# Splitting the mask pass of a top-p attention kernel between VectorE and GpSimd on Trainium2

## The chip, the cores and the metric

The kernel runs on one core of a Trainium2 chip. The metric is the device time of one execution in microseconds (us). Three runs of the kernel before took 1435.52, 1439.35 and 1441.99 us, so the median is 1439.35 us. Engines carry the names that the profile gives them: PE (TensorE), PEld (its weight loads), DVE (VectorE), ACT (ScalarE), POOL (GpSimd), SP (the queue of the loads).

## The reference, cut to what matters

```python
def top_p_attention(X, W1, W2, W3):          # X: 3327 x 128
    logits = (X @ W1.T @ W2.T) @ (X @ W3.T).T
    probs = softmax(logits)                  # 3327 x 3327
    # keep the largest probabilities of a row until their sum reaches 0.9
    keep_sorted = cs - sp < 0.9              # sp sorted, cs its running sum
    A = probs * mask
    return A / max(A.sum(-1), 1e-12)

R = row-normalised (adj + identity)
for n in range(2):                           # steps one and two
    A  = top_p_attention(Xa, W1, W2, W3)
    Xf = R @ Xf ;  Xa = A @ Xa
    Z += Xf @ U1[n].T + Xa @ U2[n].T
h = X + Z ; layer norm with gain and bias ; x + that ; layer norm
```

## The kernel before, in words

The 3327 rows are padded to 3328 and cut into 26 tiles of 128 rows; two tiles make a pair, so there are 13 pairs in each of the two steps (in the code `s` is 0 or 1, `p` the pair, `t` the tile, `x` or `xx` the tile within the pair). A tile of attention holds 128 x 3328 numbers in fp32. Two buffers `E01` and, in step one, a third hold pairs of such tiles.

**The life of a pair.** PE computes the logits in 7 chunks of up to 512 columns (line 550) and ACT stores them in `E` (line 667). DVE takes the 8 largest of each run of columns (line 833), gets the row's maximum and posts it (line 858). ACT then replaces candidates and rows by exponentials (lines 686 and 691) and posts `e_ready`. On this DVE's `search` (lines 913 to 1018) looks for the threshold `TSTAR` of each row among the candidates; while it waits for its own results it already takes the maxima of the next pair. It needs some 30 us to `TSTAR` (line 987). Where rows of a pair could not be settled (a flag tells), `level` (line 1036) reads the tiles again; that is the case for pairs 0, 5, 6, 8, 9 and 10 of step two. Before the masks, DVE finishes the next pair's maxima, so that ACT can start on the next pair's exponentials.

**The masks.** `settle` (line 1218) does this for both tiles of a pair: in step two four `match_replace` of 832 columns each (line 1232) put zeros in place of surplus ties, then one `scalar_tensor_tensor` over all 3328 columns (line 1234) multiplies the numbers by "at or above `TSTAR`", adds up what it keeps into `SUM`, and posts `a_ready`. After both tiles line 1283 takes the inverse of `SUM`.

**Units of PE's work.** PE's work is a list of units, each of 7 chunks: an A unit multiplies one masked attention tile by the features, an R unit one tile of the adjacency matrix. For each chunk PE turns up to four 128 x 128 blocks (line 595), ACT copies them out of PSUM (line 716, a ring of 3 buffers in this stage), and PE multiplies two chunks later (line 616). In step two a pair's body is A, A and then four or three R units (`STEP_R`, line 64; four for even pairs, three for odd ones, none for pair 12). The logits of pair p + 2 are made in the body of pair p, and its exponentials come at the end of that body (from step 36 on, line 166), when ACT is through with the copies before. All of this is one fixed order for each engine: an ACT instruction that waits holds everything that ACT does after it.

**Work that is spread out.** When the last unit of a pair of output tiles is done, the layer norms of these two tiles start: 6 rounds, one for each following unit (`norm_rounds`, lines 181 to 193). ACT does its half of a round at chunk 2 of the unit (lines 794 to 796), POOL its half in `norm_round` (line 485) after `add_part` of the unit before. ACT's round 0 waits for `h_taken`, that is for POOL's `add_part` (line 479) of the unit that ended the pair (line 757); a later round waits for POOL's half of the round before (line 759).

The units around the pairs that matter here, as the planner numbers them: pair 6 has its A units at 69 and 70. Before them stand the R units 66, 67 and 68. At chunk 2 of unit 68 ACT has round 4 of output pair 0 and round 0 of output pair 1; unit 67 is the one that ended output pair 1. Pair 10 has its A units at 91 and 92, with the R units 88, 89 and 90 before them; at chunk 2 of unit 90 ACT has round 4 of output pair 7 and round 0 of output pair 8, which unit 89 ended. For the even pair 8 (units 80 and 81) unit 79 has no round 0. For the odd pairs 7 and 11 a round 0 stands in the unit before the A units as well (units 74 and 96, after units 73 and 95). At chunk 0 of unit 102, the first A unit of pair 12, ACT has round 2 of output pair 11, which waits for POOL's round 1 (seven instructions, lines 493 to 499).

POOL's own program follows the units in their order (lines 510 to 520): the identity is added to the next R tile (`add_diagonal`, line 441), then the unit's result is saved (step one) or added (`add_part`), then its rounds come.

Of the kernel before, what the change touches and what calls it, by code (L numbers as in the profile page):

```python
# [6 lines left out]
def gnn_top_p_kernel(nc, x, adj, W1, W2, W3, U1, U2, ln_g, ln_b, out):  # L7
# [6 lines left out]
    P = 128  # L14
# [32 lines left out]
    MATCH = 4  # L47
    MW = NP // MATCH
    SLOTS = PARTS * 8
    SUB = 16  # L50
# [6 lines left out]
    QW = NP // QUARTERS  # L57
    HALF = [NP // 2, N - NP // 2]


# [119 lines left out]

    ROUNDS = 6
    LATE_EVERY = 3
    norm_rounds = {}
# [6 lines left out]
    for k in sorted(norm_rounds):  # L190
        norm_rounds[k].sort(key=lambda job: (job[1] if k > last_part.k else 0))
        for job in norm_rounds[k]:
            norm_at[job] = len(norm_at)
    a_unit = {(u.s, u.t): u for u in units if u.kind == "A"}

# [12 lines left out]
    with ctx:  # L208
# [6 lines left out]
        def sem(name):  # L215
            return ctx.enter_context(nc.semaphore(name))
# [62 lines left out]
        part = sb("part", [P, 2, SUB])  # L279
        st = sb("st", [P, 64])  # L280
        mv = sb("mv", [P, NT])
        sd = sb("sd", [P, NT])
# [42 lines left out]
        e_ready = sem("e_ready")  # L325
        a_ready = sem("a_ready")
        diag_ready = sem("diag_ready")
        blk_ready = sem("blk_ready")
# [87 lines left out]
        def _(pool):  # L416
# [68 lines left out]
            def norm_round(p, r):  # L485
# [14 lines left out]
                elif r == 2:  # L500
# [4 lines left out]
                    pool.tensor_tensor(h, h, X0[:, t, 0:D], ALU.add).then_inc(pool_round, 1)  # L505

            add_diagonal(r_units[0])
            add_diagonal(r_units[1])
            pool.wait_ge(h_loaded, 48)
            for u in units:  # L510
                if u.kind == "R" and 1 < u.n + 1 < 2 * NT and u.n + 1 != START_R:
                    add_diagonal(r_units[u.n + 1])
                if u.kind == "A" and u.s == 0 and u.t == NT - 1:
                    add_diagonal(r_units[START_R])
                if u.turned:
                    save(u)
                elif u.k <= last_part.k:
                    add_part(u)
                    for job in norm_rounds.get(u.k + 1, ()):
                        norm_round(*job)  # L520

        @block.tensor
        def _(pe):
# [286 lines left out]
        def _(dve):  # L810
# [49 lines left out]
            class Chain:  # L860
# [15 lines left out]

            (Z, DROPZ, THR, LOW, PICK, BUDGET, LOWW, ROOM, TSTAR, GAP, SLOW, S2, FLOOR, FLOOR2, TIE, TOTAL, TIES, CUT,
             LO, HI, WIDTH, L2, TN, GN, COUNT, LEAST, STEP, SUM, COARSE_LO, NEXT) = range(30)

            def two(n):  # L880
# [31 lines left out]

            def search(link, s, par):
                n = NC[s]
# [272 lines left out]
            for s in range(STEPS):  # L1187
                runs.finish()
                for p in range(NPAIR):
# [9 lines left out]
                    link = Chain(s_search, runs, fill, 8 if s else 0)  # L1199
                    search(link, s, par)  # L1200

# [15 lines left out]

                    def settle():

                        link = Chain(s_tie)  # L1220
                        if s:
                            link(v.tensor_tensor(gone[:, :, :, :], rank[:, :, :, :],
                                                 excess[:, :, :].rearrange("p x (n a) -> p x n a", a=1).to_broadcast([P, 2, MATCH, 8]),
                                                 ALU.is_le))
                            flat = "p x n k -> p x (n k)"
                            link(v.tensor_tensor(gone[:, :, :, :].rearrange(flat), gone[:, :, :, :].rearrange(flat),
                                                 wide(two(TSTAR), 8 * MATCH), ALU.mult))
                        for xx in range(2):
                            if s:
                                for k in range(MATCH):  # L1230
                                    back = e[:, xx, k * MW:(k + 1) * MW][:, ::-1]
                                    link.post(v.match_replace(back, gone[:, xx, k, :], back, 0.0))  # L1232
                                dve.wait_ge(s_tie, link.n)
                            v.scalar_tensor_tensor(out=e[:, xx, :], in0=e[:, xx, :], scalar=one(TSTAR, xx), in1=e[:, xx, :],  # L1234
                                                   op0=ALU.is_ge, op1=ALU.mult, accum_out=one(SUM, xx)).then_inc(a_ready, 1)

# [5 lines left out]
                    with dve.If(code > 0):  # L1242
                        if s:
# [27 lines left out]
                            with dve.If(left > 0):  # L1271
                                by_tile()
                                settle()
                        else:
# [70 lines left out]
```

## Time and profile before

| what | value |
|---|---|
| median of three runs | 1439.35 us |
| the profiled execution's own time | 1437.9 us |
| its span in the trace | 1436.1 us |
| PE busy | 1229.3 us (86%) |
| DVE busy | 1288.7 us (90%) |
| ACT busy | 921.2 us (64%) |
| POOL busy | 354.1 us (25%) |
| chain that ended last, by engine | PE 44%, DVE 37%, ACT 11%, issue 5%, POOL 1% |

Times in the trace are in us from the start of the span. "Idle before" is an engine's idle time ahead of an instruction, and the name behind the arrow is what ended it. The chain that ended last is followed back from the last instruction.

### The profile page before, as it was taken

To read this page: it belongs to the slowest core of one execution; us is meant where nothing else is said; L and a number is where in the kernel's file an instruction comes from. 1 tells how busy PE (TensorE), PEld (TensorE's weight loads), DVE (VectorE), ACT (ScalarE), POOL (GpSimd) and SP (SyncE) were. 2 spreads that over 40 slices of the span, in tenths; PEclk is the share of its full clock that TensorE was granted. 3 is DMA by queue.
4 is the path that set the end of the run, shared out by engine and by line. 5 is a ranking of instruction groups with operands and counts; after the bars stand their busy time and mean duration, and the time that the engine had idled before them with its cause. 6 is when DMAs were issued, how large, how long until landed. Compare 5 with 4: busy or idle time off the path is not lost.

```text
span 1436.1 us, 29717 instructions
## 1 busy us (share of the span) xinstructions
PE 1229.3 (86%) x9162; PEld 1037.9 (72%) x9162; DVE 1288.7 (90%) x7002; ACT 921.2 (64%) x1974; POOL 354.1 (25%) x584
## 2 busy tenths in 40 slices
PE   7899999999997989997999796919894965929896
PEld 3677777777785977887888786818784765828796
DVE  5799889988984898999989999899999998999995
ACT  4887888788757555755575655636664635636764
POOL 0221232123200341313141220202332312312242
PEclk9999999999998999998999898959997997969998
DMA  5000000000021440412132131211412031211311
GB/s 204 1 2 2 2 2 2 2 2 2 2 97 48 151 184 11 182 49 96 54 139 96 48 134 60 97 48 49 144 49 96 16 129 49 86 59 50 144 49 48
DMA packets 16599, 96.49 MB, mean 67 GB/s; under 512 B 1251, under 2 KB 8930, under 8 KB 9730
## 3 DMA queue, kind: packets, MB, share of 16 engines
q1 hardware_dynamic: 16384, 94.14, 18.6%
q8 instruction: 72, 1.18, 0.3%
q14 instruction: 143, 1.17, 0.3%
HBM read 92.43 MB, written 1.70 MB: 66 GB/s over the span
## 4 chain that ended last, share of the span: by engine, by line
PE 44%; DVE 37%; ACT 11%; issue 5%; POOL 1%; DVEq 1%; DMA 0%; SPq 0%; ACTq 0%; POOLq 0%
PE bank L616 25%; DVE cand L833 13%; PE bank L595 11%; DVE junkC L890 8%; PE bank L550 5%; ACT E L691 4%; DVE E L1232 2%; ACT blkT L716 2%; ACT cand L686 2%; DVE sub L1054 2%; DVE E L1234 1%; PE bank L631 1%; DVE junkS L890 1%; DVE slots L953 1%; ACT S L691 1%
## 5 line engine op out<-in xcount | busy, mean ns | idle before, releaser
L716 ACT ACTIVATE blkT<-bank 128x512 f32<-128x512 f32 (+1 forms) x728 | 406.7, 565 | 283.0 <-PE bank L595 279.0
L833 DVE MAX8 cand<-E 128x8 f32<-128x32 f32 (+1 forms) x2992 | 404.4, 192 | 37.2 <-ACT E L667 22.7
L616 PEld LDWEIGHTS bank<-X,blkT 128*128 128x128 f32 x2704 | 330.3, 192 | 107.8 <-ACT blkT L716 76.3
L616 PE MATMUL bank<-X,blkT 128*128 128x129 f32 (+1 forms) x2704 | 377.5, 282 | 13.9 <-ACT blkT L716 12.7
L595 PE MATMUL bank<-ident,S 128*128 128x128 f32 x1560 | 243.3, 276 | 16.0 <-POOL S L447 14.2
L595 PE MATMUL bank<-ident,E 128*128 128x128 f32 x1144 | 182.1, 284 | 81.9 <-DVE E L1234 81.9
L890 DVE SCALAR_TENSOR_TENSOR junkC<-cand,st 128x128 f32<-128x128 f32 (+2 forms) x390 | 241.1, 626 | 2.4
L616 PE MATMUL bank<-YF,blkT 128*128 128x128 f32 x1352 | 193.0, 287 | 43.1 <-ACT blkT L716 43.1
L616 PEld LDWEIGHTS bank<-YF,blkT 128*128 128x128 f32 x1352 | 172.5, 199 | 74.7 <-ACT blkT L716 63.6
L550 PE MATMUL bank<-kT,Q 64*128 64x512 f32 (+1 forms) x728 | 197.2, 614 | 7.9 <-ACT E L667 7.6
L595 PEld LDWEIGHTS bank<-ident,E 128*128 128x128 f32 x1144 | 142.8, 148 | 84.0 <-DVE E L1234 82.8
L595 PEld LDWEIGHTS bank<-ident,S 128*128 128x128 f32 x1560 | 187.2, 143 | 21.1 <-POOL S L447 16.3
L667 ACT ACTIVATE E<-bank 128x512 f32<-128x512 f32 (+1 forms) x308 | 158.0, 567 | 57.0 <-PE bank L550 56.7
L616 PE MATMUL bank<-YA,blkT 128*128 128x128 f32 x1352 | 185.5, 280 | 0.5 <-ACT blkT L716 0.5
L616 PEld LDWEIGHTS bank<-YA,blkT 128*128 128x128 f32 x1352 | 170.5, 197 | 1.0 <-ACT part_h L737 0.7
L1234 DVE SCALAR_TENSOR_TENSOR E<-E,st 128x3328 f32<-128x3328 f32 x44 | 163.0, 3721 | 8.8 <-DVE flag_i L1031 6.8
L691 ACT ACTIVATE E<-E,negm 128x1664 f32<-128x1664 f32 x88 | 147.4, 1675 | 0.0
L476 POOL TENSOR_TENSOR H<-hy,H 128x128 f32<-128x128 f32 x26 | 37.9, 1456 | 283.7 <-ACT hy L752 283.7
L1232 DVE MATCH_REPLACE8 E<-gone,E 128x832 f32<-128x832 f32 x104 | 103.8, 1009 | 0.0
L686 ACT ACTIVATE cand<-cand,negm 128x520 f32<-128x520 f32 (+1 forms) x78 | 44.9, 591 | 90.7 <-DVE negm L858 90.7
L550 PEld LDWEIGHTS bank<-kT,Q 64*128 64x128 f32 x728 | 56.8, 186 | 42.9 <-issue 27.4
L483 POOL TENSOR_TENSOR H<-part_h,H 128x128 f32<-128x128 f32 x50 | 33.2, 664 | 190.1 <-ACT part_h L737 190.0
(222 smaller groups left out, 1336.2 us busy)
## 6 DMA issues: line engine op xcount, KB each, us to landing
S<-in_adj_dram SPq DMA_DIRECT2D x50, 1663.5 KB, 7.0
S<-in_adj_dram SPq DMA_DIRECT2D x2, 1455.6 KB, 8.1
X<-in_x_dram SPq DMA_DIRECT2D x6, 256.0 KB, 4.1
out_dram<-H SPq DMA_DIRECT2D x1, 1408.0 KB
S<-in_adj_dram SPq DMA_DIRECT2D x2, 194.9 KB, 9.9
u_in<-in_L_gnn_U_dram SPq DMA_DIRECT2D x4, 64.0 KB, 9.5
out_dram<-H SPq DMA_DIRECT2D x1, 128.0 KB
w_in<-in_L_gnn_W_dram SPq DMA_DIRECT2D x2, 32.0 KB, 2.0
```

What stands on the lines that cost most here:

```text
L476: pool.tensor_tensor(H[:, u.t, :], hy[:, z, 0:D], H[:, u.t, :], ALU.add)
L550: pe.matmul(lg_banks(q)[xx][:, 0:LW[c]], Q[h0:h1, p, :], kT[h0:h1, s, c * BANK:c * BANK + LW[c]], start=True, stop=True).then_inc(logits_r ...
L595: m = pe.transpose(BLK[early][slot][:, b * P:(b + 1) * P], src[:, j * P:(j + 1) * P], ident[:, :])
L616: m = pe.matmul(bank[int(u.acc)][:, 0:width], blkT[:, slot, b * P:(b + 1) * P], rhs[:, j, 0:width], start=(j == 0), stop=(j == NT - 1))
L667: act.activation(E[where_e[s, p]][:, xx, c * BANK:c * BANK + LW[c]], lg_banks(q)[xx][:, 0:LW[c]], ACT.Copy).then_inc(logits_done, 1)
L686: act.activation(c, c, ACT.Exp, bias=negm[:, par, xx:xx + 1], scale=1.0, accum_out=total[:, par, xx:xx + 1])
L691: return act.activation(e[:, xx, lo:hi], e[:, xx, lo:hi], ACT.Exp, bias=negm[:, par, xx:xx + 1], scale=1.0, accum_out=Zh[:, par, xx, half: ...
L716: act.activation(blkT[:, slot, 0:w], BLK[early][slot][:, 0:w], ACT.Copy).then_inc(blk_done, 1)
L833: v.max(cand[:, par, xx, 8 * r:8 * r + 8], E[where_e[self.s, self.p]][:, xx, r * w:min((r + 1) * w, N)]).then_inc(s_max, 1)
L890: return v.scalar_tensor_tensor(out=out, in0=a, scalar=limit, in1=a, op0=ALU.is_lt, op1=ALU.mult, accum_out=total)
L1232: link.post(v.match_replace(back, gone[:, xx, k, :], back, 0.0))
L1234: v.scalar_tensor_tensor(out=e[:, xx, :], in0=e[:, xx, :], scalar=one(TSTAR, xx), in1=e[:, xx, :], op0=ALU.is_ge, op1=ALU.mult, accum_out= ...
```

## The change

In step two, POOL masks the last 320 columns (`EW`) of each tile, with two instructions and a buffer `over`; DVE masks the first 3008. DVE does the `match_replace` of the last quarter first and posts `end_cleaned` with it. PE waits for `end_masked` at chunk 5 of an A unit, the first that touches these columns. DVE waits for the masks of the pair before ahead of writing `TSTAR` again. In POOL's program `mask_ends(p)` stands two units ahead of the pair's first A unit, between that unit's `add_diagonal` and its save or `add_part`. The kept sum is no longer added up by the mask pass: it is the row's mass minus the allowed drop, minus the gap, minus the ties taken out. A fallback for rows that `level` leaves open keeps adding up (`settle(False)`). Step one stays as it was.

```diff
+    EW = 5 * P // 2
...
+    MASKS_AHEAD = 2
...
+    masks_before = {a.k - MASKS_AHEAD: a.pair for a in units if a.kind == "A" and a.s and a.x == 0}
...
+            def mask_ends(p):
+                for t in (2 * p, 2 * p + 1):
+                    pool.wait_ge(end_cleaned, t + 1)
+                    last = E[where_e[1, p]][:, t % 2, NP - EW:]
+                    limit = st[:, 2 * TSTAR + t % 2:2 * TSTAR + t % 2 + 1]
+                    if t:
+                        pool.wait_ge(end_masked, t)
+                    then(pool.tensor_scalar(over[:, :], last, limit, None, ALU.is_ge))
+                    pool.tensor_tensor(last, last, over[:, :], ALU.mult).then_inc(end_masked, 1)
...
             for u in units:
                 if u.kind == "R" and 1 < u.n + 1 < 2 * NT and u.n + 1 != START_R:
                     add_diagonal(r_units[u.n + 1])
+                if u.k in masks_before:
+                    mask_ends(masks_before[u.k])
...
+                if u.s and u.kind == "A" and c == (NP - EW) // BANK:
+                    pe.wait_ge(end_masked, u.t + 1)
...
+                if s and p:
+                    dve.wait_ge(end_masked, 2 * p)
                 link(v.tensor_reduce(two(TSTAR), d, AX.X, ALU.min))
...
+                        link.post(v.tensor_tensor(two(SUM), two(Z), two(DROPZ), ALU.subtract))
...
+                            for k in (MATCH - 1, *range(MATCH - 1)):
                                 back = e[:, xx, k * MW:(k + 1) * MW][:, ::-1]
+                                ins = v.match_replace(back, gone[:, xx, k, :], back, 0.0)
+                                if k < MATCH - 1 or not counted:
+                                    link.post(ins)
+                                else:
+                                    ins.then_inc(end_cleaned, 1)
+                                if xx == 0 and counted:
+                                    if k == 0:
+                                        link.post(v.tensor_tensor(two(SUM), two(SUM), two(GAP), ALU.subtract))
+                                        link.post(v.tensor_reduce(two(S2), gone[:, :, :, :].rearrange(flat), AX.X, ALU.add))
+                                        total_at = link.n
+                                    elif k == 1:
+                                        dve.wait_ge(s_tie, total_at)
+                                        link.post(v.tensor_tensor(two(SUM), two(SUM), two(S2), ALU.subtract))
+                            dve.wait_ge(s_tie, link.n)
...
+                            ins = v.scalar_tensor_tensor(out=e[:, xx, 0:end], in0=e[:, xx, 0:end], scalar=one(TSTAR, xx),
+                                                         in1=e[:, xx, 0:end], op0=ALU.is_ge, op1=ALU.mult,
+                                                         accum_out=None if counted else one(SUM, xx))
+                            ins.then_inc(a_ready, 1)
```

## Rows read from the trace of the kernel before

**Rows 1.** Window, length; busy us (count) of PE, PEld, DVE, ACT, POOL; clock; DMA.

```profile
805.00:1290.00 485.00, 358.65 (x2743) 317.47 (x2743) 456.85 (x2627) 269.60 (x611) 113.77 (x222) 0.87 0.21 75
```

**Rows 2.** Waits, same stretch: waiter, awaited, us in total, times, longest.

```profile
ACT cand L686 <- DVE negm L858: 82.3, 5, 22.9
...
PE bank L595 <- DVE E L1234: 77.0, 3, 31.2
```

**Rows 3.** Timeline of DVE, pair 6: start, us, engine, line, operation, operands.

```profile
966.23 1.01 DVE L1232 MATCH_REPLACE8 E<-gone,E 128x832 f32<-128x832 f32 x1
...
970.25 3.69 DVE L1234 SCALAR_TENSOR_TENSOR E<-E,st 128x3328 f32<-128x3328 f32 x1
...
974.66 0.17 DVE L931 TENSOR_SCALAR st<-st 128x2 f32<-128x2 f32 x1
974.73 0.16 DVE L932 TENSOR_SCALAR st<-st 128x2 f32<-128x2 f32 x1
```

**Rows 4.** Timeline of PE at the start of unit 69.

```profile
966.29 2.82 PE L595 MATMUL bank<-ident,E 128*128 128x128 f32 x12 [31.18 <-DVE E L1234]
```

**Rows 5.** Timeline of ACT at the end of pair 6's body.

```profile
1040.38 0.19 ACT L691 ACTIVATION_READ_ACCUMULATOR E<-E,negm 128x1 f32 x1
```

**Rows 6.** Timeline of DVE at the start of the search for pair 8.

```profile
1040.71 0.16 DVE L929 TENSOR_TENSOR st<-Zh 128x2 f32<-128x2 f32 x1
```

**Rows 7.** Groups of DVE by shape: line, names, shapes, count, busy us, mean ns.

```profile
L890 DVE SCALAR_TENSOR_TENSOR junkC<-cand,st 128x832 f32<-128x832 f32 x104 | 113.0, 1096 | 1.3
```

**Rows 8.** Timeline of POOL: 128 columns, the first beside a mask pass of DVE.

```profile
603.22 3.30 POOL L471 TENSOR_SCALAR scaled<-hy,row_inv 128x128 f32<-128x128 f32 x1 [3.64 <-ACT hy L752]
...
658.88 0.46 POOL L472 TENSOR_TENSOR H<-scaled,H 128x128 f32<-128x128 f32 x1
659.32 0.60 POOL L473 TENSOR_SCALAR YF<-hy,row_inv 128x128 f32<-128x128 f32 x1
```

**Rows 9.** Timeline of POOL: a two-input instruction of 256 columns.

```profile
984.22 0.73 POOL L504 TENSOR_TENSOR H<-H,gb 128x256 f32<-128x256 f32 x1
```

**Rows 10.** Timeline of DVE at 602 us.

```profile
602.35 3.69 DVE L1234 SCALAR_TENSOR_TENSOR E<-E,st 128x3328 f32<-128x3328 f32 x1
```

**Rows 11.** Timeline of ACT: unit 68, chunk 2, then pair 7's exponentials.

```profile
931.93 0.31 ACT L764 ACTIVATE u_in<-H 128x128 f32<-128x128 f32 x1
...
932.53 0.85 ACT L716 ACTIVATE blkT<-bank 128x512 f32<-128x512 f32 x2
...
957.30 0.84 ACT L686 ACTIVATE cand<-cand,negm 128x520 f32<-128x520 f32 x1 [21.72 <-DVE negm L858]
```

**Rows 12.** Timeline of POOL: add_part of unit 67.

```profile
927.88 0.46 POOL L483 TENSOR_TENSOR H<-part_h,H 128x128 f32<-128x128 f32 x1 [4.15 <-ACT part_h L737]
```

**Rows 13.** Timeline of PE at the lower clock.

```profile
1023.55 1.92 PE L616 MATMUL bank<-YF,blkT 128*128 128x128 f32 x8
```

**Rows 14.** Timeline of ACT around pair 4: exponentials, then the fifth copy.

```profile
795.14 0.84 ACT L686 ACTIVATE cand<-cand,negm 128x520 f32<-128x520 f32 x1
...
804.37 0.19 ACT L691 ACTIVATION_READ_ACCUMULATOR E<-E,negm 128x1 f32 x1
...
810.55 0.60 ACT L716 ACTIVATE blkT<-bank 128x512 f32<-128x512 f32 x1 [0.73 <-PE bank L595]
```

**Rows 15.** Timeline of ACT: the fifth copy of unit 69.

```profile
973.33 0.60 ACT L716 ACTIVATE blkT<-bank 128x512 f32<-128x512 f32 x1 [1.02 <-PE bank L595]
```

**Rows 16.** Timeline of ACT: the fifth copy of unit 91.

```profile
1295.66 0.60 ACT L716 ACTIVATE blkT<-bank 128x512 f32<-128x512 f32 x1 [0.73 <-PE bank L595]
```

**Rows 17.** The chain that ended last, in order of time: start, us, what.

```profile
1286.23 3.71 DVE E L1234 x2
1289.98 2.82 PE bank L595 x12
```

**Rows 18.** Timeline of ACT at the end of pair 10's body.

```profile
1361.07 0.19 ACT L691 ACTIVATION_READ_ACCUMULATOR E<-E,negm 128x1 f32 x1
```

**Rows 19.** Timeline of ACT: round 2 of output pair 11.

```profile
1408.13 0.88 ACT L768 ACTIVATE H<-H,shift,rs 128x128 f32<-128x128 f32 x2
```

More of the change, by code:

```diff
@@ L58, in gnn_top_p_kernel @@
     HALF = [NP // 2, N - NP // 2]
+    (Z, DROPZ, THR, LOW, PICK, BUDGET, LOWW, ROOM, TSTAR, GAP, SLOW, S2, FLOOR, FLOOR2, TIE, TOTAL, TIES, CUT,
+     LO, HI, WIDTH, L2, TN, GN, COUNT, LEAST, STEP, SUM, COARSE_LO, NEXT) = range(30)
     START_R, TURN_R = 2, 8
@@ L280, in gnn_top_p_kernel @@
         st = sb("st", [P, 64])
+        over = sb("over", [P, EW])
         mv = sb("mv", [P, NT])
@@ L326, in gnn_top_p_kernel @@
         a_ready = sem("a_ready")
+        end_cleaned = sem("end_cleaned")
+        end_masked = sem("end_masked")
         diag_ready = sem("diag_ready")
@@ L875, in __call__ @@
                     dve.wait_ge(self.sem, self.n)
-            (Z, DROPZ, THR, LOW, PICK, BUDGET, LOWW, ROOM, TSTAR, GAP, SLOW, S2, FLOOR, FLOOR2, TIE, TOTAL, TIES, CUT,
-             LO, HI, WIDTH, L2, TN, GN, COUNT, LEAST, STEP, SUM, COARSE_LO, NEXT) = range(30)
             def two(n):
@@ L911, in smallest_kept, with search @@
                 return w, d
-            def search(link, s, par):
+            def search(link, s, p, par):
                 n = NC[s]
@@ L1199, in _ @@
                     link = Chain(s_search, runs, fill, 8 if s else 0)
-                    search(link, s, par)
+                    search(link, s, p, par)
                     if p + 1 < NPAIR:
@@ L1216, in by_tile, with settle @@
                                 drop_ties(e, xx)
-                    def settle():
+                    def settle(counted=True):
                         link = Chain(s_tie)
[L1221 to L1227, printed above, removed]
-                        for xx in range(2):
[L1229 to L1235, printed above, removed]
@@ new lines, in settle @@
+                        if not s:
+                            for xx in range(2):
+                                v.scalar_tensor_tensor(out=e[:, xx, :], in0=e[:, xx, :], scalar=one(TSTAR, xx), in1=e[:, xx, :],
+                                                       op0=ALU.is_ge, op1=ALU.mult, accum_out=one(SUM, xx)).then_inc(a_ready, 1)
+                            return
+                        link(v.tensor_tensor(gone[:, :, :, :], rank[:, :, :, :],
+                                             excess[:, :, :].rearrange("p x (n a) -> p x n a", a=1).to_broadcast([P, 2, MATCH, 8]),
+                                             ALU.is_le))
@@ new lines, in settle @@
+                        flat = "p x n k -> p x (n k)"
+                        link.post(v.tensor_tensor(two(SUM), two(Z), two(DROPZ), ALU.subtract))
+                        link(v.tensor_tensor(gone[:, :, :, :].rearrange(flat), gone[:, :, :, :].rearrange(flat),
+                                             wide(two(TSTAR), 8 * MATCH), ALU.mult))
+                        end = NP - EW
+                        for xx in range(2):
+                            for k in (MATCH - 1, *range(MATCH - 1)):
+                                back = e[:, xx, k * MW:(k + 1) * MW][:, ::-1]
+                                ins = v.match_replace(back, gone[:, xx, k, :], back, 0.0)
[12 more added lines that the diff above has]
+                            dve.wait_ge(s_tie, link.n)
+                            if not counted:
+                                last = e[:, xx, end:]
+                                link(v.scalar_tensor_tensor(out=junkC[:, 0, 0:EW], in0=last, scalar=one(TSTAR, xx), in1=last,
+                                                            op0=ALU.is_ge, op1=ALU.mult, accum_out=one(S2, xx)))
+                                v.tensor_copy(w8[:, 0, 0:1], one(S2, xx)).then_inc(end_cleaned, 1)
+                            ins = v.scalar_tensor_tensor(out=e[:, xx, 0:end], in0=e[:, xx, 0:end], scalar=one(TSTAR, xx),
+                                                         in1=e[:, xx, 0:end], op0=ALU.is_ge, op1=ALU.mult,
+                                                         accum_out=None if counted else one(SUM, xx))
+                            ins.then_inc(a_ready, 1)
@@ L1238, in _ @@
+                        if not counted:
+                            dve.wait_ge(a_ready, 2 * gp + 2)
+                            link(v.tensor_tensor(two(SUM), two(SUM), two(S2), ALU.add))
                     with dve.If(code < 1):
@@ L1272, in _ @@
                                 by_tile()
-                                settle()
+                                settle(False)
                         else:
```

## Prediction

> **What bounds the kernel now.** I read the page first: DVE has the largest busy share (90%), PE follows with 86%, and the chain that ended last gives PE 44% and DVE 37%. Such a mixture needs stages. The window from 805 to 1290 us shows DVE busy for 456.85 of 485 us and PE for 358.65 [rows 1], and the waits there name DVE twice: ACT waits for its row maxima, PE for its masks, 77.0 us in three waits [rows 2]. One of these is pair 6: I call the end of the mask pass over its first tile T6 = 966.23 us, where the second tile's first match_replace starts; the second mask pass starts at T6 + 4.0, and small instructions there follow each other at 0.07 us [rows 3]. PE had been idle for 31.18 us and starts unit 69 at T6 + 0.1 [rows 4]. But DVE is not the bound everywhere. Pair 8's search could not start before pair 8's exponentials: ACT's last one ends at 1040.57 us [rows 5], the search's first instruction comes at 1040.71 us [rows 6]. So from T6 to 1040.7 us PE and ACT, working through pair 6's body, set the pace together with DVE. What delays that body delays everything after it.
>
> **DVE's own part.** A mask-like pass over 832 columns takes 1.096 us [rows 7], one over 3328 takes 3.69 us [rows 3]. The slope is 2.59 / 2496 = 1.04 ns a column, so 320 columns fewer give back 0.33 us a tile, 0.67 us a pair. Added per pair are three two-column instructions and one reduction over 64 columns: at the spacing of 0.07 us of [rows 3] and about 0.19 us for the reduction (an estimate from that spacing and the slope) 0.4 us. They stand among the match_replaces, so nothing hides them. The accumulator read that goes had the next instruction's start beside it: nothing. Net gain 0.27 us a pair; I take 0.2, because POOL now reads SBUF beside them. It counts only where DVE sets the pace: some five pairs, so **1.0 us**; the bounds are 13 x 0.67 = 8.7 us gained, and a loss if POOL's instructions hold up DVE's passes.
>
> **POOL's part.** A one-input instruction of 128 columns takes 0.60 us, a two-input one 0.46 us [rows 8], one of 256 columns 0.73 us [rows 9], so 2.1 ns a column. For 320 columns: the comparison between 1.0 (that slope) and 1.5 us (in proportion), taken as 1.2; the product 0.73 + 64 x 0.0021 = 0.86, taken as 0.9. Beside a mask pass POOL does not get on: the instruction of 603.22 us lasted 3.30 us instead of about 0.6 and ended 0.5 us after DVE's pass, which ran from 602.35 to 606.04 us [rows 8, 10]. For the second tile of a pair POOL has the match_replaces' time: released at T + 1.0, comparison done at T + 2.3, product at T + 3.3, before the next pass begins at T + 4.0. Should it miss, that tile is done some 5 us later.
>
> The Trainium skill (SBUF — State Buffer, section "SBUF: two separate sides") says that a DVE instruction with two SBUF inputs and a GpSimd instruction that reads SBUF exclude each other for their whole length, whichever came first. The 3.30 us agree for DVE coming first. By that rule DVE can lose as well, up to 0.9 us at each pass that finds POOL's product under way. No row above needs it, and the sum would be up to 5 us higher with it.
>
> **What stands behind POOL's new wait.** `mask_ends(p)` stands two units ahead of the pair's A units and waits for DVE's settle of *both* tiles, until T + 3.3. Everything behind it in POOL's program is held: the `add_part` of that unit and of the next, the rounds, the next `add_diagonal`. For pairs 0 to 4 those are saves with two slots in hand and nobody needs them before the second unit after. For pair 6 the held `add_part` is that of unit 67, now done at 928.34 us [rows 12], long before T6. ACT's round 0 of output pair 1, at chunk 2 of unit 68, needs exactly that one; ACT does it at 931.93 us, copies two more chunks, and after a wait of 21.72 us for DVE's maxima begins pair 7's exponentials at 957.30 us [rows 11]. They end just at T6 + 0.3, hidden behind DVE. **After the change ACT stands at that round from 932 us until T6 + 3.9, and the exponentials, hidden before, come after it.** There is no ring: DVE has the logits of pair 7 by then.
>
> Step by step from T6 (times as T6 + ...): add_part 0.46 us after the product, done at 3.9; round 0 takes 0.6 us (931.93 to 932.53 us), 4.6; two copies 0.85, 5.4 [rows 11]. PE has two multiplies of unit 68 left; after 30 us of idling I take the lower clock, 1.92 us for a whole chunk [rows 13] and half of that for the last one, of two blocks: 7.9. ACT stores the sums, 0.4: 8.3. Exponentials of a pair in one go, with nothing in between: 795.14 to 804.56 us, 9.4 us, and the fifth copy of the next A unit 6.0 us after that [rows 14]. So pair 7's exponentials are ready at 17.7, and the fifth copy of unit 69 starts at 23.7. Now that copy starts at 973.33 us, at T6 + 7.1 [rows 15]. The body of pair 6 is late by **16.6 us**, its end with pair 8's exponentials too, and since the search for pair 8 waits for them now with 0.1 us in hand, DVE is late by as much from there on. DVE itself is late only 9.5 us at its search for pair 7, so it does not add to this.
>
> Pair 10 is the same picture: unit 89's `add_part` is held, round 0 of output pair 8 waits for it at chunk 2 of unit 90. There the fifth copy of unit 91 starts at 1295.66 us [rows 16]; T10 is 1286.23 + 3.69 = 1289.92 us, where the chain goes over from DVE to PE [rows 17], so the copy is at T10 + 5.7 now and at T10 + 23.7 then: **18.0 us**. Pair 12's exponentials, now through at 1361.26 us [rows 18], move along, and from here PE's units set the end.
>
> The other pairs. Pair 8: no round 0 before its A units, only late rounds at unit 80, some 5 us of ACT; the wait for maxima later in that body takes them up. Pairs 7 and 11: round 0 is held there as well, but with their bodies already 17 us late, and DVE only 10, ACT comes to it after POOL is through. Pair 12: round 2 of output pair 11 starts at 1408.13 us [rows 19], T12 + 4.1; POOL's seven instructions before it would now be blocked by the second pass, and end near T12 + 9.8. ACT and PE are late by then themselves, and the ring covers two chunks: **1.5 us** stay (between 0 and 5.5).
>
> **Sum.** The profiled execution took 1437.9 us, 1.45 less than the median of the three runs shown. 1437.9 - 1.0 + 16.6 + 18.0 + 1.5 = **1473.0 us**, some 2.4% slower. On the median it would be 1474.5; I keep 1473.
>
> **The rivals.**
> *Only one of the two stalls costs its full size, or each half* (PE at full clock, the body takes some back, the DVE wait that follows swallows it). For it: pair 6's body has waits of its own. Against: the exponentials alone are 9.4 us and nothing can hide them. 1437.9 + 18 = 1456 us. Chance 0.11.
> *POOL misses its gap.* Part of the forecast's range: two times 5 us more, 1483 us.
> *ACT is not held*: the round's add comes in time, or the round is not where I read it. Then DVE's small gain and POOL's contention remain: 1437 us, within 0.5%. Chance 0.09. *With DVE's passes held up by POOL* in the same case, the second tile of all 13 pairs x 0.9 us, less the gain: 1437.9 + 11.7 - 1 = 1448.6 us. Chance 0.05.
> *The other side, faster*: DVE sets the pace in all 13 pairs, the added instructions vanish in its waits, and POOL is always back before ACT comes; it decides once ACT reaches the round no earlier than T + 3.9. 1437.9 - 8.7 = 1429 us. For it: DVE's 90%. Against: ACT came 34 us before T6 [rows 11], and pair 8's search waited for ACT [rows 5, 6]. Chance 0.03.
> *That the change doesn't do what it says*: with `a_ready` after 3008 columns, PE could be stopped at chunk 5 instead. It gets there 6 us after its start, POOL is through at T + 3.3; nothing from this.
>
> The Trainium skill (GPSIMD Engine Reference, section "Engine selection") advises against elementwise work with two inputs on GpSimd, at about half of DVE's speed. The 2.1 ns against 1.04 ns a column agree; the forecast does not rest on it.
>
> **How the numbers follow.** The forecast, both stalls, has 0.72, from 1464 us (PE at full clock, quicker POOL) to 1488 us (POOL misses both gaps). With the rival of one stall it has 0.83; the range 1455 to 1489 us takes both in and leaves the rest out. A measurement can tell about 0.5%, 7.2 us, from no change. Faster by more: 0.03. Within: 0.09. Slower: 0.72 + 0.11 + 0.05 = 0.88.
>
> **What would show it.** Right: in the chain of waits and the waits of ACT, one at line 757's round (the identity-with-sum activation on `H`) for POOL's `add_part`, of some 38 us at pair 6 and 30 us at pair 10; pair 7's and pair 11's exponentials after the masks of pairs 6 and 10, not before; DVE waiting about 9.5 us at `search`'s first instruction in both; fifth copies at T + 23.7; the mask pass at 3.35 us; POOL's pair of instructions 2.1 us beside match_replaces. Wrong: exponentials of pair 7 before T6, or PE starting unit 69 within 1 us of T6. A POOL product that starts only after the second pass says that POOL missed its gap. If DVE's passes stay at 3.35 us but start late, the contention rival holds.

## The result, and the profile after

| | before | after |
|---|---|---|
| median of 4 runs each, on the same chip | 1439.09 us | **1482.57 us** |
| ratio of the two, 95% interval | | 1.0311 [1.0295, 1.0326] |
| the profiled execution's own time | 1437.9 us | 1482.74 us |
| its span | 1436.1 us | 1481.0 us |

The change makes the kernel 3.1% slower; the forecast of 1473.0 us was 9.6 us too low and its range held the time. Between the profiled executions lie 1482.74 - 1437.9 = 44.8 us. Line numbers of after are higher than those of before: L644 (multiplies) was L616, L744 (copies of transposed blocks) L716, L719 (exponentials) L691, L792 and L794 (ACT's rounds) L764 and L766, L623 (blocks turned) L595, L954 (the search's first instruction) L929, L459 (`add_diagonal`) L447, L495 (`add_part`) L483, L505 to L511 (round 1) L493 to L499, L1285 (mask pass) L1234. POOL's two mask instructions are L527 and L528.

The waits from 805 to 1350 us; columns: engine, its tile and line, what it waited for, us in total, times, longest.

```profile
PE bank L644 <- ACT blkT L744: 129.1, 15, 37.2
...
ACT u_in L792 <- POOL H L495: 73.1, 2, 37.9
...
ACT cand L714 <- DVE negm L886: 42.7, 3, 22.8
DVE st L954 <- ACT E L719: 31.0, 3, 11.4
...
PE bank L623 <- DVE E L1285: 19.2, 1, 19.2
...
PE bank L623 <- POOL S L459: 11.5, 7, 5.0
```

ACT (L792) waits twice for POOL's add (L495), which before it never did in this stretch, and PE waits behind ACT where it had waited for DVE's masks [rows 2]. One PE wait for DVE's masks is left of three. DVE now waits for the exponentials: 31.0 us in three waits here, 42.5 us in four up to the end.

Pair 6 in the timelines of POOL, ACT, PE and DVE (start, us, engine, line, operation, operands, and in brackets the idle time before and what ended it).

```profile
966.07 1.08 POOL L527 TENSOR_SCALAR over<-E,st 128x320 f32<-128x320 f32 x1 [5.60 <-DVE E L1265]
967.23 0.86 POOL L528 TENSOR_TENSOR E<-E,over 128x320 f32<-128x320 f32 x1
968.05 0.45 POOL L495 TENSOR_TENSOR H<-part_h,H 128x128 f32<-128x128 f32 x1
```

```profile
968.54 0.31 ACT L792 ACTIVATE u_in<-H 128x128 f32<-128x128 f32 x1 [37.87 <-POOL H L495]
...
972.79 0.37 ACT L765 ACTIVATE part_h<-bank,row_inv 128x128 f32<-128x128 f32 x1 [2.81 <-PE bank L644]
...
982.28 0.19 ACT L719 ACTIVATION_READ_ACCUMULATOR E<-E,negm 128x1 f32 x1
...
988.55 0.60 ACT L744 ACTIVATE blkT<-bank 128x512 f32<-128x512 f32 x1 [1.92 <-PE bank L623]
```

```profile
931.55 1.06 PE L644 MATMUL bank<-YF,blkT 128*128 128x128 f32 x8
969.77 2.93 PE L644 MATMUL bank<-YF,blkT 128*128 128x128 f32 x12 [37.16 <-ACT blkT L744]
...
983.10 2.05 PE L644 MATMUL bank<-YA,blkT 128*128 128x128 f32 x8 [8.05 <-ACT blkT L744]
```

```profile
964.96 1.01 DVE L1265 MATCH_REPLACE8 E<-gone,E 128x832 f32<-128x832 f32 x1
...
968.98 3.35 DVE L1285 SCALAR_TENSOR_TENSOR E<-E,st 128x3008 f32<-128x3008 f32 x1
...
982.61 0.16 DVE L954 TENSOR_TENSOR st<-Zh 128x2 f32<-128x2 f32 x1 [9.80 <-ACT E L719]
```

T6, where the second tile's first match_replace starts, is 964.96 us. POOL's comparison starts at T + 1.1, its product ends at T + 3.1, the add at T + 3.5; ACT, which had come to its round at 930.7 us (968.54 less the wait of 37.87), starts it at T + 3.6. The exponentials of pair 7 follow the store of the sums at 972.79 us and end at 982.47 us, T + 17.5. Before, they were over at 966.72 us, T + 0.5, as this row of ACT in the kernel before shows:

```profile
966.53 0.19 ACT L691 ACTIVATION_READ_ACCUMULATOR E<-E,negm 128x1 f32 x1
```

DVE waits 9.80 us for them, and the fifth copy of unit 69 starts at 988.55 us = **T + 23.6**, where it was at T + 7.1 [rows 15]. At pair 10, with T10 = 1310.99 us, the same: the round at 1314.57 us, the fifth copy at 1333.96 us.

### The profile page after: what moved, and what is told of

It reads as the page before. It is cut to its first block, busy times and chain, and to the rows that moved or that the text cites. A ratio compares the mean times of both kernels' runs of the same rounds, so it can differ in the third digit from the quotient of the medians.

```text
span 1481.0 us, 29858 instructions
## 1 busy us (share of the span) xinstructions
PE 1238.0 (84%) x9162; PEld 1043.5 (70%) x9162; DVE 1285.5 (87%) x7028; ACT 919.5 (62%) x1974; POOL 415.1 (28%) x636
## 4 chain that ended last, share of the span: by engine, by line
PE 44%; DVE 35%; ACT 13%; issue 5%; POOL 2%; DVEq 1%; DMA 0%; SPq 0%; ACTq 0%; POOLq 0%
PE bank L644 25%; DVE cand L861 13%; PE bank L623 11%; DVE junkC L915 7%; PE bank L575 5%; ACT E L719 5%; DVE E L1265 2%; ACT blkT L744 2%; ACT cand L714 2%; DVE E L1285 2%; DVE sub L1081 2%; PE bank L659 1%; DVE junkS L915 1%; ACT S L719 1%; DVE st L925 1%
## 5 line engine op out<-in xcount | busy, mean ns | idle before, releaser
L744 ACT ACTIVATE blkT<-bank 128x512 f32<-128x512 f32 (+1 forms) x728 | 405.6, 564 | 290.1 <-PE bank L623 286.1
L644 PEld LDWEIGHTS bank<-X,blkT 128*128 128x128 f32 x2704 | 329.8, 192 | 107.7 <-ACT blkT L744 75.4
L644 PE MATMUL bank<-X,blkT 128*128 128x129 f32 (+1 forms) x2704 | 376.8, 281 | 12.3 <-ACT blkT L744 11.1
L644 PE MATMUL bank<-YF,blkT 128*128 128x128 f32 x1352 | 196.7, 291 | 113.6 <-ACT blkT L744 113.5
L644 PEld LDWEIGHTS bank<-YF,blkT 128*128 128x128 f32 x1352 | 175.5, 202 | 145.8 <-ACT blkT L744 134.7
L623 PE MATMUL bank<-ident,S 128*128 128x128 f32 x1560 | 244.2, 277 | 21.9 <-POOL S L459 20.2
L623 PEld LDWEIGHTS bank<-ident,S 128*128 128x128 f32 x1560 | 187.8, 143 | 27.2 <-POOL S L459 22.3
L644 PE MATMUL bank<-YA,blkT 128*128 128x128 f32 x1352 | 188.3, 283 | 19.6 <-ACT blkT L744 19.6
L623 PE MATMUL bank<-ident,E 128*128 128x128 f32 x1144 | 181.9, 283 | 24.0 <-DVE E L1285 24.0
L644 PEld LDWEIGHTS bank<-YA,blkT 128*128 128x128 f32 x1352 | 172.8, 199 | 21.1 <-issue 17.2
L623 PEld LDWEIGHTS bank<-ident,E 128*128 128x128 f32 x1144 | 143.2, 148 | 25.7 <-DVE E L1285 24.5
L719 ACT ACTIVATE E<-E,negm 128x1664 f32<-128x1664 f32 x88 | 147.4, 1677 | 0.0
L1285 DVE SCALAR_TENSOR_TENSOR E<-E,st 128x3008 f32<-128x3008 f32 x26 | 87.9, 3382 | 0.9
L527 POOL TENSOR_SCALAR over<-E,st 128x320 f32<-128x320 f32 x26 | 28.2, 1086 | 213.5 <-DVE E L1265 213.1
```

Of the source, the lines that this page charges most:

```text
L623: m = pe.transpose(BLK[early][slot][:, b * P:(b + 1) * P], src[:, j * P:(j + 1) * P], ident[:, :])
L644: m = pe.matmul(bank[int(u.acc)][:, 0:width], blkT[:, slot, b * P:(b + 1) * P], rhs[:, j, 0:width], start=(j == 0), stop=(j == NT - 1))
L719: return act.activation(e[:, xx, lo:hi], e[:, xx, lo:hi], ACT.Exp, bias=negm[:, par, xx:xx + 1], scale=1.0, accum_out=Zh[:, par, xx, half: ...
L744: act.activation(blkT[:, slot, 0:w], BLK[early][slot][:, 0:w], ACT.Copy).then_inc(blk_done, 1)
L1285: ins = v.scalar_tensor_tensor(out=e[:, xx, 0:end], in0=e[:, xx, 0:end], scalar=one(TSTAR, xx), in1=e[:, xx, 0:end], op0=ALU.is_ge, op1=AL ...
```

## What the later pairs add

From the fifth copy to the last exponential of pair 8 (1059.22 us, T + 94.3, for T + 74.3) the loss since T6 grows from 16.5 to 19.9 us. This remainder arises behind the stall, where pair 7's masks are made, seen at POOL, DVE and PE.

```profile
1035.34 0.19 POOL L505 TENSOR_SCALAR sd<-sd 128x2 f32<-128x2 f32 x1 [4.62 <-ACT u_in L794]
...
1036.40 3.20 POOL L507 TENSOR_TENSOR newton<-rs 128x2 f32<-128x2 f32 x1
...
1040.66 0.45 POOL L459 TENSOR_TENSOR S<-S,ident 128x128 f32<-128x128 f32 x1
1041.10 1.09 POOL L527 TENSOR_SCALAR over<-E,st 128x320 f32<-128x320 f32 x1
...
1044.48 3.23 POOL L528 TENSOR_TENSOR E<-E,over 128x320 f32<-128x320 f32 x1
```

```profile
1036.20 3.35 DVE L1285 SCALAR_TENSOR_TENSOR E<-E,st 128x3008 f32<-128x3008 f32 x1
...
1043.57 3.42 DVE L1285 SCALAR_TENSOR_TENSOR E<-E,st 128x3008 f32<-128x3008 f32 x1
...
1059.36 0.16 DVE L954 TENSOR_TENSOR st<-Zh 128x2 f32<-128x2 f32 x1 [11.43 <-ACT E L719]
```

```profile
1041.17 1.11 PE L623 MATMUL bank<-ident,S 128*128 128x128 f32 x4 [5.02 <-POOL S L459]
1042.08 1.91 PE L644 MATMUL bank<-YF,blkT 128*128 128x128 f32 x8
...
1046.34 1.07 PE L644 MATMUL bank<-YF,blkT 128*128 128x128 f32 x8
```

The shift has put POOL's round 1 beside DVE's mask pass. The third of its seven two-column instructions takes 3.20 us instead of 0.20 and ends 0.05 us after the pass; `add_diagonal` behind it comes at 1040.66 us, and PE stands 5.02 us for it. In the kernel before, with round 1 running free, that wait was 2.02 us:

```profile
1022.97 0.79 PE L595 MATMUL bank<-ident,S 128*128 128x128 f32 x4 [2.02 <-POOL S L447]
```

PE's next multiplies in the changed kernel run at the lower of TensorE's two clocks (granted clock 0.51 from 1039.5 to 1046.4 us; 1.91 us for a chunk, 1.07 us else). And POOL, late, starts pair 7's second product only beside the second mask pass: 3.23 us. At pair 11 all of this comes again (a wait of 5.02 us, ended at 1386.58 us).

So the 44.8 us, each term rounded: -1.3 up to T6 (DVE), +16.5 pair 6, +3.5 pair 7's body, +2.4 from there to T10, +17.2 at pair 10 (fifth copy at T + 23.0 for T + 5.7), +5.1 in pair 11's body, +1.4 pair 12 and the end.

## The experiments

Twelve kernels. Each ratio is to the kernel before in interleaved runs; before itself had medians from 1437.02 to 1437.66 us there.

**Masks one unit ahead** (`e1_ahead1`).

```
-    MASKS_AHEAD = 2
+    MASKS_AHEAD = 1
```

> The change, with POOL's masks one unit later (one unit ahead of the A units instead of two), so that the add_part which ACT's round 0 waits for comes before them. Theory (the held add_part is the cost): ACT's two waits of 38 and 35 us for POOL are gone, the exponentials of pairs 7 and 11 lie beside the masks of pairs 6 and 10 again, and the time is that of the kernel before less DVE's small gain, 1435 to 1440 us. Rival one (POOL's 52 instructions themselves, or their contention with DVE's passes, are the cost): 1470 us or more. Rival two (a wait takes the old one's place, for the add_part of the unit right ahead of the A units): 1445 to 1455 us.

Measured: 1445.69 us, ratio 1.0058 [1.0045, 1.0072]. Both stalls are gone; ACT's waits for `add_part` from 805 to 1350 us add up to 0.3 us:

```profile
PE bank L623 <- DVE E L1285: 83.2, 3, 30.9
...
ACT u_in L792 <- POOL H L495: 0.3, 1, 0.3
```

Against the runs of the kernel before that each was compared with, the loss falls from 43.5 us (1482.57 for 1439.09) to 8.6 us (1445.69 for 1437.05). One constant takes back four fifths. But I had expected 1435 to 1440 us: 8.6 us are left, and the number lies in the range of rival two, though its wait is not there (0.3 us).

**Masks two ahead, but behind the unit's own add** (`e2_add_first`): `mask_ends` stands between `add_part(u)` and the rounds.

> The change, with the masks still two units ahead, but behind that unit's add_part instead of ahead of it; the rounds and the next add_part stay held. Theory: the 35 us waits go with the add_part alone. What is left is ACT at chunk 2 of the first A unit, T + 7, waiting for POOL's seven-instruction round, which ends near T + 8.5: 1 to 2 us at pairs 6, 10 and 12 each, so 1438 to 1446 us. Rival (the held rounds matter as much as the add_part): 1455 us or more.

Measured: 1446.09 us, 1.0049 [1.0034, 1.0065]. The wait itself may stand two units ahead, if the one add that ACT needs goes first. This is just above what was expected; a loss of the same size is left, 9.0 us.

**Pair 6 alone moved** (`e3_pair6_only`): one unit ahead at pair 6, two at all others.

> The change, with the masks of pair 6 alone one unit later. Theory: pair 6's stall goes and pair 10's stays, each worth its own: pair 6's was 19 to 20 us by the two traces, so 1461 to 1465 us, with one ACT wait of some 35 us for POOL left. Rival (the stalls hang together: the first one shifts the phases and makes the second or part of it): 1440 to 1455 us.

Measured: 1462.95 us, 1.0173 [1.0157, 1.0188]. The two places add up: between the profiled executions lie 1482.74 - 1463.12 = 19.6 us for pair 6 with what it does to pair 7 (19.9 us by the trace of the change), and the rest is pair 10's.

**DVE's half alone** (`e4_dve_only`): `mask_ends` and its waits go, DVE's mask pass has its full width again, the kept sum still comes from the row's mass.

```
-  ins = v.scalar_tensor_tensor(out=e[:, xx, 0:end], in0=e[:, xx, 0:end], ...
+  to = NP if counted else end
+  ins = v.scalar_tensor_tensor(out=e[:, xx, 0:to], in0=e[:, xx, 0:to], ...
```

> DVE's half of the change alone: the kept sum comes from the row's mass, the last quarter's match_replace comes first, but DVE masks all 3328 columns and POOL masks nothing. Theory: no stall at all; the three small instructions and the reduction cost 0.33 us a pair on DVE, so some 5 to 8 pairs x 0.33 us more than the kernel before, 1440 to 1443 us, and the mask pass stays at 3.69 us. Rival (dropping the accumulator or the new order of the sum is itself worth something): below 1438 us.

Measured: 1437.98 us, 1.0006 [0.9997, 1.0015]: no difference, where 1440 to 1443 us had been expected. The added instructions do cost DVE what was forecast (8.64 us from the start of the settling to T in nearly every pair, for 8.31), but nothing of it shows in the time.

**The wait without the masks** (`e5_wait_only`): e4, and at `mask_ends`' place a bare wait of POOL. This kernel's lines stand up to three lower than those of the change.

```
-                    mask_ends(masks_before[u.k])
+                    pool.wait_ge(end_cleaned, 2 * masks_before[u.k] + 2)
```

> The DVE half of the change alone (full-width mask passes by DVE, as in e4_dve_only, 1438.0 us), plus a bare wait on GpSimd two units ahead of each pair, for the first match_replace of the pair's second tile, with no mask behind it. My theory: ACT's stall at round 0 comes from the order of GpSimd's program, not from its masks. GpSimd gets on at T + 1.0 instead of T + 3.3, so each of the two stalls is about 2.3 us shorter than in the changed kernel, and the late diagonals of pairs 7 and 11 stay: 1482.6 - 2 x 2.3 + 1 = 1479 us, expected 1474 to 1481; ACT's wait for the add of GpSimd about 35.6 us at pair 6. Rival (the masks themselves and their share of SBUF make up the loss): 1438 to 1450 us.

Measured: 1476.18 us, 1.0272 [1.0256, 1.0288]. ACT's longest wait for the add is 36.6 us with nothing masked on POOL:

```profile
PE bank L641 <- ACT blkT L741: 122.9, 13, 35.9
...
ACT u_in L789 <- POOL H L495: 71.2, 3, 36.6
```

That is as expected. The wait's place alone is 39.2 of the 43.5 us (1476.18 - 1437.02 of 1482.57 - 1439.09). The order of POOL's program makes nine tenths of the loss, not its masks.

**The other side of the queue** (`e6_rounds_later`): POOL waits as in the change; ACT's and POOL's rounds of output pairs 1 and 8 begin one unit later.

```
-  norm_rounds.setdefault(min(u.k + 1 + r, last_part.k + 1), []).append((u.pair, r))
+  norm_rounds.setdefault(min(u.k + 1 + r + (u.pair in (1, 8)), last_part.k + 1), []).append((u.pair, r))
```

> The changed kernel with its masks two units ahead as they are, and the normalization rounds of output pairs 1 and 8 begun one unit later, so that ACT's round 0 of them no longer stands ahead of the exponentials of pairs 7 and 11 while GpSimd holds the add. My theory: both stalls go though GpSimd waits as long as before: 1438 to 1447 us (what is left is the gain of 1 us, and whatever the later rounds find in their new places), and the exponentials of pair 7 end before T of pair 6. Rival (PE or DVE is held by GpSimd's long wait in another way as well, by the next diagonal or the ring): above 1455 us.

Measured: 1445.44 us, 1.0057 [1.0041, 1.0072]. POOL waits 35.88 us, as in the change, and ACT isn't held by it: the last of pair 7's exponentials is over at 964.70 us, T + 0.4 (T6 is 964.27 us here), the same as in the kernel before (966.63 us; the read of its sum ends 0.1 us later). I had written before T. Round 0 comes at 973.83 us.

```profile
957.75 1.09 POOL L527 TENSOR_SCALAR over<-E,st 128x320 f32<-128x320 f32 x1 [35.88 <-DVE E L1265]
...
967.37 0.46 POOL L495 TENSOR_TENSOR H<-part_h,H 128x128 f32<-128x128 f32 x1
```

```profile
963.03 1.67 ACT L719 ACTIVATE E<-E,negm 128x1663 f32<-128x1663 f32 x1
...
973.83 0.31 ACT L792 ACTIVATE u_in<-H 128x128 f32<-128x128 f32 x1
```

**Round 1 away from the mask pass** (`e12_round_one_later`): the changed kernel, rounds 1 to 5 of output pairs 2 and 9 one unit later (the edit of e6 with `r > 0 and u.pair in (2, 9)`).

> The changed kernel, in which rounds 1 to 5 of output pairs 2 and 9 come one unit later. My theory for the 3.4 us that each stall cost beyond the forecast: GpSimd's seven small instructions of round 1 fall beside DVE's mask pass of pair 7 (and 11), one of them lasts 3.2 us, the next diagonal is late, and PE waits 5.0 instead of 2.0 us for it. With the round gone from there PE's wait is back at 2 us or less at both places, and the time falls by 3 to 7 us: 1475.5 to 1479.5 us. Rival (the extra time is the clock's, or ACT's order in the body): 1481 to 1484 us.

Measured: 1472.66 us, 1.0235 [1.0216, 1.0254], 9.9 us less than the change, where 3 to 7 us had been expected (9.5 us between the profiled executions). `add_diagonal` comes right behind `add_part` now, before the pass, and PE's wait for it is gone:

```profile
1029.36 0.46 POOL L495 TENSOR_TENSOR H<-part_h,H 128x128 f32<-128x128 f32 x1 [3.03 <-ACT part_h L765]
1033.39 0.46 POOL L459 TENSOR_TENSOR S<-S,ident 128x128 f32<-128x128 f32 x1 [3.57 <-ACT H L796]
...
1044.55 1.88 POOL L505 TENSOR_SCALAR sd<-sd 128x2 f32<-128x2 f32 x1 [1.98 <-ACT u_in L794]
...
1047.32 0.20 POOL L507 TENSOR_TENSOR newton<-rs 128x2 f32<-128x2 f32 x1
```

```profile
1039.96 0.60 PE L623 MATMUL bank<-ident,S 128*128 128x128 f32 x4
```

Counted from T6 and T10, pair 7's body ends 7.3 us earlier, pair 11's 6.4 us; 2.0 us of the first are given back before T8. That is more than the 3.0 us by which PE's wait had grown: the whole wait of 5.02 us goes, and of the two stretches at the lower clock (1039.5 to 1046.4 and 1056.6 to 1063.4 us) one of 3.4 us is left. It is also more than the 3.5 and 5.1 us that the change had lost there. Between the fifth copy and the last exponential pair 7's body takes 67.2 us before, 70.7 in the change and 63.4 here, pair 11's 65.6, 70.7 and 63.6. So e12 shows that the loss there hangs on round 1's place, but it also takes away what round 1 costs the kernel before (the wait of 2.02 us and 3.4 us at the lower clock behind it), and how much of the 8.6 us is round 1's alone it doesn't measure.

### What is left of the loss when the stalls are gone

e1, e2 and e6 all end at 1445 to 1446 us, by different ways. Two kernels tested whether that is made at pair 12, where POOL's round 1, its masks and round 2 come one after another: **pair 12 masked by DVE** (`e7_not_last_pair`), and **pair 12's masks two units ahead** (`e8_last_pair_early`), all others one ahead.

> As e1_ahead1 (masks one unit ahead of the pair, 1445.7 us), and the last pair is masked by DVE over its full width, without GpSimd. My theory: e1's loss is made in pair 12 and behind it, where GpSimd's round 1, its masks and round 2 of output pair 11 come one after another, twice held by a DVE pass, and ACT and PE wait for them with nothing in between. Without pair 12's masks that goes, and the small gain of DVE shows: 1436 to 1440 us, the same as the kernel before (1437 us) within what a measurement can tell. Rival (the loss of e1 comes from the sum of small delays at all pairs): 1443 to 1446 us.

> Masks one unit ahead of pairs 0 to 11, two units ahead of pair 12, where the changed kernel lost only 1.0 us behind pair 12. If e1's loss lies in GpSimd's order around pair 12, with the masks behind round 1: 1438 to 1442 us. If any mask of pair 12 by GpSimd costs as much wherever it stands: 1445 us and more, since round 2 of output pair 11 is late behind the second mask pass in either order.

Measured: 1443.33 us, 1.0040 [1.0027, 1.0054], and 1447.85 us, 1.0069 [1.0055, 1.0083]. My theory falls, and each number lies in the range of its rival. In pair 12 and behind it e1 does have a wait that e7 has not (from 1364 to 1440 us, e1 first, e7 second):

```profile
ACT u_in L792 <- POOL H L517: 5.7, 1, 5.7
```

```profile
ACT u_in L792 <- POOL H L517: 2.1, 1, 2.1
```

Before has 1.8 us there. But e7 is only 2.4 us below e1: it is 5.3 us behind the kernel before already at the start of pair 11's unit 97, where e1 is 1.8 us behind and then loses 5.2 us more. The delays stand in several places and change places from kernel to kernel, as the rival has it. So the masks were taken out of e1 with POOL's wait left in place (`e9_wait_one_ahead`). DVE masks the full width again, and the waits of PE and DVE for `end_masked` go with the masks; in e1 neither engine ever waited for POOL's product, so those waits cost nothing there.

> e1_ahead1 without its masks: GpSimd waits one unit ahead of each pair for the first match_replace of the pair's second tile and does nothing there, DVE masks the full width. It tells what the loss of e1 (1445.7 us) is made of. Theory A (the masks on GpSimd hold DVE up: in e1's profile DVE's instructions after the first pair are 22.5 us longer in all than the median of their form, against 15.8 us before; and they hold the rounds up): 1438 to 1441 us, and that excess back at about 16 us. Theory B (the place of the wait, the add held by it): 1443 to 1446 us.

Measured: **1438.65 us, 1.0004 [0.9994, 1.0014]**. Theory A: it is the masks on POOL. One way in which they cost shows at pair 9 of e1, at DVE and POOL:

```profile
1208.06 1.01 DVE L1265 MATCH_REPLACE8 E<-gone,E 128x832 f32<-128x832 f32 x1
1209.11 3.80 DVE L1285 SCALAR_TENSOR_TENSOR E<-E,st 128x3008 f32<-128x3008 f32 x1
...
1213.97 0.85 DVE L959 TENSOR_SCALAR st<-st 128x2 f32<-128x2 f32 x1
```

```profile
1207.71 1.10 POOL L527 TENSOR_SCALAR over<-E,st 128x320 f32<-128x320 f32 x1
1208.89 0.87 POOL L528 TENSOR_TENSOR E<-E,over 128x320 f32<-128x320 f32 x1
1209.93 3.92 POOL L527 TENSOR_SCALAR over<-E,st 128x320 f32<-128x320 f32 x1 [0.18 <-POOL E L528]
1213.94 0.86 POOL L528 TENSOR_TENSOR E<-E,over 128x320 f32<-128x320 f32 x1
```

Late by its own add, POOL meets the second mask pass: DVE's pass is held by the product (3.80 us for 3.35), the next comparison by the pass (3.92 for 1.1), and the product after it holds a two-column instruction of the next search (0.85 us for 0.16). Add up, over all DVE instructions from 450 us on that took more than 0.12 us above the median of their line, operation and shape, what they took above it: 16.5 us before, 23.8 us in e1, 16.1 us in e9 (the expectation above has somewhat lower figures, 15.8 and 22.5, for the first two). The 7.3 us more are larger than the gain of 13 x 0.35 = 4.6 us, and e1 is 3.3 us late at T12. Another 3.7 us are lost behind it, where ACT waits 5.7 us for POOL's round. That is not the whole account, though: in e6, and in the two kernels below, the same sum is 20.8, 20.5 and 20.5 us, 4.0 to 4.3 us above that of before and so no more than the gain, and yet they are 5.6 to 8.4 us slower. The rest must lie in waits for POOL's later rounds and adds, which I haven't split; e9 shows that without the masks it is gone.

**Two tries at a version that wins**: `e10_only_two_moved` (one unit ahead at pairs 6 and 10 alone), and `e11_last_on_dve` (that, and pair 12 masked by DVE).

> The changed kernel with the masks one unit ahead at pairs 6 and 10 alone, two units ahead at all others. If the two stalls are all that makes the change slow, and the masks beside match_replaces cost DVE less than those of e1: 1437 to 1441 us, ACT's long waits gone at both places, and e1's loss at pairs 7 to 9 smaller. If the end (pair 12 and the last rounds) costs as in e8: 1443 to 1447 us.

> As e10, and pair 12 masked by DVE over its full width. The candidate to beat both: what is gained at DVE (1 to 2 us by pair 6 in every run so far) and nothing of the end. Expected 1436 to 1441 us; faster than the kernel before by more than 0.5% would need 1430 us, which I give 1 in 20.

Measured: 1444.09 us, 1.0038 [1.0024, 1.0053], and 1443.27 us, 1.0034 [1.0023, 1.0046]. e10 lies in the second of its ranges (the end costs as in e8), e11 missed. By pair 6, e11 is 1.3 us ahead of before, as the change is; at the start of pair 11's unit 97 it is 4.5 us behind, of which 3.6 us came since T11 (1355.78 us for 1354.85). There it is the change's stall over again, small (POOL, ACT, PE of e11):

```profile
1358.06 0.86 POOL L528 TENSOR_TENSOR E<-E,over 128x320 f32<-128x320 f32 x1
1358.87 0.46 POOL L495 TENSOR_TENSOR H<-part_h,H 128x128 f32<-128x128 f32 x1
```

```profile
1359.36 0.31 ACT L792 ACTIVATE u_in<-H 128x128 f32<-128x128 f32 x1 [2.76 <-POOL H L495]
```

```profile
1362.26 3.15 PE L644 MATMUL bank<-YF,blkT 128*128 128x128 f32 x12 [5.21 <-ACT blkT L744]
```

The masks two units ahead of pair 11 hold an add that ACT's round 0 of output pair 10 needs; ACT waits 2.76 us, and PE 5.21 us where it had waited 2.53. Putting pair 11 one unit ahead too was not tried in this kernel (in e7, where it stands so, the same unit comes 5.3 us late); even 3.6 us off 1443.3 would leave it at 1439.7, above the kernel before. No version run with masks on POOL came below the kernel before, and e4 and e9, level with it, mask nothing there.

## Why the prediction was right, and by what it was short

- **DVE's own part**: forecast a gain of 0.27 us a pair, taken as 0.2, 1.0 us in all. From the start of the settling to the second tile's first match_replace it is 8.30 us for 8.31, where the shorter pass just pays for the added instructions, and from there to the inverse of `SUM` 7.68 us for 8.02: 0.35 us a pair, and 1.3 us by T6. The mask pass takes 3.35 us, as forecast.
- **POOL's part**: forecast 2.1 us, released at T + 1.0; measured 1.08 + 0.86 us, released at T + 1.1. It reached its gap at pairs 6 and 10, as forecast; it missed it at pairs 7 and 11 (a product of 3.23 us each), which I had not looked at.
- **ACT held**: forecast waits of 38 and 30 us; measured 37.87 and 35.23 us. The second was misread by 5 us; that moves nothing, since what counts is when the wait ends. Shown by e5 and e6: the wait without masks makes it, and rounds moved away from it unmake it.
- **Step by step from T6**: PE's two multiplies done (7.9 forecast, 972.70 us = 7.7 measured), exponentials ready (17.7; 17.5), the fifth copy (23.7; 23.6), DVE's wait at the search (9.5; 9.8). 16.6 us forecast, **16.5 us** measured. Pair 10: 18.0 and **17.2 us**. Pair 12: 1.5 and 1.4 us; round 1 was held by the second pass as forecast, and ACT waited 2.76 us for it. One reading was off: before, pair 7's exponentials end at T6 + 0.5 and not + 0.3, which moves no term of the sum.
- **The step that fell short** is "what delays that body delays everything after it": it took the bodies behind as moved whole. Counted from T6, POOL, ACT and PE moved by 16 us, DVE's masks of the same body by 9.5, since DVE had been ahead. So POOL's rounds met DVE passes that they had missed before. The loss there is 3.5 + 5.1 us; e12 shows that round 1's place matters by moving it, though not its exact share. The prediction had looked at pairs 7 and 11 for a second wait of ACT only. 2.4 us more, between pair 8 and pair 10, I can't assign.
- **The range** held the time partly by luck: its upper end of 1488 us had been made for POOL missing its gaps at pairs 6 and 10, which it didn't, and what filled that room was a loss that the prediction didn't have.
- **The rivals**: one stall alone is what e3 built, and it gives 1463.0 us, the rival's 1456 us plus the extra in pair 11's body and the end; with both places as they are, both stalls came in full. DVE held by POOL with no stall is seen in e1: 1445.7 us, where the rival had 1448.6 us. The number is near and the way is not: the rival had 0.9 us at the second tile of all 13 pairs, while in e1 only three of the 26 mask passes took over 0.1 us more (3.46, 3.62 and 3.80 us), and half of its loss comes behind T12. The Trainium skill (SBUF — State Buffer, section "SBUF: two separate sides") has it that a DVE instruction with two SBUF inputs and a GpSimd instruction that reads SBUF exclude each other, and that whichever starts first blocks the other for its whole length. The rows of pair 9 in e1 agree in both directions: 3.80 us for DVE's pass behind a product, 3.92 us for POOL's comparison behind that pass.

## What to carry to other kernels

A wait that is put into an engine's program is paid by the one that needs what stands behind it, not by what the wait is for; here an add of 0.45 us, held for 35 us, cost 17 us on an engine that had nothing to do with the masks. Look through everything queued behind the new wait and ask of each item who needs it next. After a stall, engines don't move together: look again at which work now falls beside which. And take work to POOL only where its instructions fall beside work of DVE that doesn't exclude them: in e1 the 4.6 us gained on DVE were less than the 7.3 us by which its instructions grew, and what came later on POOL cost ACT and PE more still.

## What was not expected of the hardware

Beside match_replaces nothing is lost on either side: 1.01 us for DVE (its usual time), 1.08 and 0.86 us for POOL [after, pair 6]. Beside a mask pass POOL's smallest instruction, two columns, goes from 0.20 to 3.20 us. And DVE's smallest is held too: a product of POOL of 0.86 us made a two-column instruction with one input last 0.85 us instead of 0.16 [e1, pair 9]. In these rows the size of an instruction doesn't tell what it costs there. Not tried: the edit of e12 on the kernel before, where PE waits 2.02 us behind round 1 and a row of POOL at pair 7, 4.04 us long for 256 columns (0.73 us for the two before it), is held in the same way:

```profile
1035.74 4.04 POOL L505 TENSOR_TENSOR H<-H,X 128x256 f32<-128x256 f32 x1
```
